# A graph and expert kernel: weights loaded during the projection, gathers of 128 rows, edge rows stored in two parts, six x buffers, the last group in halves

## What is computed

```python
h = rmsnorm(layernorm(x)) * rms_w @ W_down          # 10000 x 256
src, dst = edges + one loop per node
xl, xr = h @ Wl, h @ Wr                             # 4 heads of 64
e = sum(leaky(xl[src] + xr[dst]) * att)             # per edge and head
alpha = softmax of e over the edges with the same dst
x = x + segment_sum(alpha * xl[src], dst) @ W_up
z = layernorm(x)
w[i] = mean(top2(z @ expert_tokens.T) == i)         # 0 or 1/2 for each of 8 experts
x = x + sum_i w[i] * (gelu(gelu(z @ W1[i] + b1[i]) @ W2[i] + b2[i]) @ W3[i] + b3[i])
```

## Time and profile before

| what | us |
|---|---|
| runs shown | 1731.69, 1720.94, 1732.09 (median 1731.69) |
| profiled execution, its own time | 1720.88 |
| its span, first to last instruction | 1719.2 |
| PE busy | 1541.9 (90%) |
| DVE busy | 1201.9 (70%) |
| ACT busy | 687.1 (40%) |
| POOL busy | 692.5 (40%) |

### The profile page before, as it was taken

How to read it: one execution, slowest core, us unless ns; L and a number is a source line. 1 busy time by engine, 2 the same in 40 slices (tenths; PEclk the granted TensorE clock), 3 DMA queues, 4 the chain that set the end, 5 groups by cost and what they waited for, 6 DMA issues and landing times.

```text
span 1719.2 us, 29202 instructions
## 1 busy us (share of the span) xinstructions
PE 1541.9 (90%) x9481; PEld 1280.2 (74%) x9481; DVE 1201.9 (70%) x2392; ACT 687.1 (40%) x1365; POOL 692.5 (40%) x720
## 2 busy tenths in 40 slices
PE   6999999995697645999999992999999999999997
PEld 5999999994486334888787781777777777777775
DVE  5666666663487664887788785677777777777775
ACT  2444444442243630000000000666666666666663
POOL 1121112114677003565555536344444444444432
PEclk9999999997799886898889886999999999999999
DMA  9766566633934146799988985677666676765420
GB/s 217 214 160 166 162 174 162 152 97 90 177 104 113 60 142 154 182 238 252 251 240 243 242 254 174 206 224 219 214 210 215 208 214 205 223 198 175 128 56 15
DMA packets 136589, 306.37 MB, mean 178 GB/s; under 512 B 78543, under 2 KB 80845, under 8 KB 129067
## 3 DMA queue, kind: packets, MB, share of 16 engines
q1 hardware_dynamic: 70235, 196.21, 43.3%
q0 software_dynamic: 66208, 108.34, 21.0%
HBM read 219.78 MB, written 138.85 MB: 209 GB/s over the span
## 4 chain that ended last, share of the span: by engine, by line
PE 42%; issue 19%; DMA 19%; POOL 7%; DVE 3%; SPq 3%; ACT 2%; ACTq 0%; POOLq 0%; DVEq 0%
DMA rows_x<-cx 13%; PE psum L1845 13%; PE psum L1813 7%; PE psum L1519 7%; PE psum L1520 5%; PE psum L1521 5%; PE psum L1843 4%; POOL xls L624 2%; POOL where_from L592 2%; POOL td L628 2%; ACT xld L845 2%; DMA w_raw<-in_L_ffn_W 1%; SPq L421 1%; SPq L431 1%; POOL rstd L581 1%
## 5 line engine op out<-in xcount | busy, mean ns | idle before, releaser
L1845 PE MATMUL psum<-w_raw,gl 128*128 128x512 f32 x528 | 269.7, 592 | 0.0
L876 ACT ACTIVATE xt_hi<-psum 128x512 fp32r<-128x512 f32 x264 | 150.6, 596 | 238.3 <-PE psum L1813 238.2
L1446 DVE TENSOR_TENSOR xt_lo<-psum,xt_hi 128x512 fp32r<-128x512 f32 x264 | 176.5, 689 | 79.7 <-ACT xt_hi L876 79.7
L1558 PE MATMUL psum<-wdx_hi,axt_hi 128*125 128x272 f32 x640 | 191.5, 299 | 7.0 <-DVE wd_lo L994 4.0
L1813 PEld LDWEIGHTS psum<-ident,xn 128*128 128x128 f32 x1056 | 126.5, 142 | 94.2 <-issue 68.3
L1459 DVE SCALAR_TENSOR_TENSOR xb<-psum,xb 128x512 f32<-128x512 f32 x264 | 176.1, 687 | 28.5 <-PE psum L1845 28.4
L960 DVE TENSOR_TENSOR axt_lo<-psum,axt_hi 128x500 fp32r<-128x500 f32 x160 | 108.5, 678 | 122.8 <-ACT axt_hi L744 122.7
L1560 PE MATMUL psum<-wdx_hi,axt_lo 128*125 128x272 f32 x640 | 185.7, 290 | 0.0
L1559 PE MATMUL psum<-wd_lo,axt_hi 128*125 128x256 f32 x640 | 180.3, 282 | 0.0
L870 ACT ACTIVATE xn<-xb 128x1024 f32<-128x1024 f32 x132 | 156.1, 1233 | 53.5 <-DMA xb<-rows_x,idx_in 53.5
L716 POOL DMA_INDIRECT out<-xb,idx_in x132 | 133.6, 1012 | 106.2 <-issue 59.7
(11 more groups left out here) (277 smaller groups left out, 3944.5 us busy)
## 6 DMA issues: line engine op xcount, KB each, us to landing
rows_x<-cx SPq DMA_DIRECT2D x20, 1806.0 KB
w_raw<-in_L_ffn_W SPq DMA_DIRECT2D x140, 256.0 KB, 12.4
cx<-in_x SPq DMA_DIRECT2D x20, 1792.0 KB
ax<-in_x SPq DMA_DIRECT2D x19, 1792.0 KB
node_table<-trow SPq DMA_DIRECT2D x19, 896.0 KB
node_table<-xld SPq DMA_DIRECT2D x10, 500.0 KB
rows_x<-cx SPq DMA_DIRECT2D x20, 209.6 KB
cx<-in_x SPq DMA_DIRECT2D x20, 208.0 KB
```

What stands on the lines that cost most here:

```text
L1446: dve.tensor_tensor(xt_lo[:, 2 * q:2 * q + 2, :].rearrange("p k n -> p (k n)"), T_R[q % 2], xt_hi[:, 2 * q:2 * q + 2, :].rearrange("p k n ...
L1558: pe.matmul(into, high, wdx_hi[:, k, :], start=k == 0, stop=False, skip_group_check=True)
L1845: pe.matmul(Y[u], gl2[:, t % 2, rows], w3_raw[:, t % N3, HALF * n:HALF * (n + 1)], start=False, stop=True, skip_group_check=True).then_inc ...
```

## The change

- w1 is loaded in eight parts in groups 1 to 8 of the projection and w_up in group 9; w1 is split on ACT and DVE in groups 11 to 18, w_up in batches 4 to 7 of the edge stage, and turned in batches 0 to 3.
- All gathers of xls, td and agg take 128 rows; the index tables have 128 partitions, the three new ones hold row 0. `pad` clears what the new partitions of the buffers may hold.
- Each pass of edge rows is stored in two parts, of 112 and of 13 partitions. dst_row is loaded after half of the batches.
- Eight masks (NSM) instead of two.
- Six cx buffers (NCX) instead of three; loads 1 to 5 are issued once the first group's agg has landed; `load_cx(g + 5)` takes the place of `load_cx(g + 2)`.
- In the group stage, `ranks_in`, `place`, `slots` and `slot_numbers` of the group before come earlier.
- The last group's moments, scale, shift and store are done in two halves.
- The memset of xb goes; two columns of all eight buffers are cleared by POOL. The memset of `tail` goes.

The diff, cut to its core:

```diff
-NOLD, NR, N3 = 4, 4, 4
+NCX, NSM = 6, 8
+NR, N3 = 4, 4
 ROW = D + 8
 SLOTS = NE - 1
 LAST_PAIR = (NE - 2) * NE + NE - 1
 SENT = 520
+PADT, PADW = 16288, 17408
...
+        cx3, cx4, agg, aggt_hi, aggt_lo, cx5, c_end = run_of(
             at3,
-            ("cx1", [P, J, ROW], F32), ("cx2", [P, J, ROW], F32), ("agg", [P, 2, J, HID], F32),
-            ("aggt_hi", [128, 2, KH, G], F32R), ("aggt_lo", [128, 2, KH, G], F32R))
+            ("cx3", [P, J, ROW], F32), ("cx4", [P, J, ROW], F32), ("agg", [128, 2, J, HID], F32),
+            ("aggt_hi", [128, 2, KH, G], F32R), ("aggt_lo", [128, 2, KH, G], F32R), ("cx5", [P, J, ROW], F32))
         at_cx0 = (nc.sbuf_usable_end - origin - J * ROW * 4) // 32 * 32
-        cx = [put("cx0", [P, J, ROW], F32, at_cx0), cx1, cx2]
+        at_cx1 = at_cx0 - J * ROW * 4
+        cx = [put("cx0", [P, J, ROW], F32, at_cx0), put("cx1", [P, J, ROW], F32, at_cx1),
+              put("cx2", [P, J, ROW], F32, at4 - J * ROW * 4), cx3, cx4, cx5]
...
+            return 32 * ((NG - b + 2) // 3 + (b == (NG - 1) % 3))
...
+            sp.dma_start(pad[P:128, 0:NAX * J * D].rearrange("p (a d) -> p a d", d=D),
+                         b3_hl[P:128, :].bitcast(F32).unsqueeze(1).broadcast_to([128 - P, NAX * J, D])
+                         ).then_inc(pad_zero, 16)
...
+                if GW1 <= g < GW1 + KD:
+                    k = g - GW1
+                    sp.dma_start(w1_raw[:, :, 1, k, :],
+                                 w1[:, 128 * k:128 * (k + 1), :].rearrange("e p h -> p e h")).then_inc(raw_w1, 16)
+                if g == GW1 + KD:
+                    sp.dma_start(wup_raw[:, :, :], w_up.rearrange("(k p) n -> p k n", p=128)).then_inc(raw_wup, 16)
...
-            sp.wait_ge(setup_v, 11)
-            sp.wait_ge(sent_put, 16 * ((PAIRS + 1) * CAP // (128 * SENT)))
-            sp.dma_start(wup_raw[:, :, :], w_up.rearrange("(k p) n -> p k n", p=128)).then_inc(raw_wc, 16)
-            for k in range(KD):
-                sp.dma_start(w1_raw[:, :, 1, k, :],
-                             w1[:, 128 * k:128 * (k + 1), :].rearrange("e p h -> p e h")).then_inc(raw_wc, 16)
             for par in range(2):
                 sp.wait_ge(t_stored[par], T_STORED[par])
-            sp.wait_ge(b_xld, NBG)
+            sp.wait_ge(b_xld, NBG // 2)
...
                 sp.wait_ge(b_out, b + 1)
-                sp.dma_start(t_edge[:, bass.ds(CB * b, CB), :], xld[:, bass.ds(CB * b, CB), :]
-                             ).then_inc(rows_stored[par], 16)
+                for rows in (slice(0, SPLIT), slice(SPLIT, P)):
+                    sp.dma_start(t_edge[rows, bass.ds(CB * b, CB), :], xld[rows, bass.ds(CB * b, CB), :]
+                                 ).then_inc(rows_stored, 16)
...
+            sp.wait_ge(rows_stored, 32 * NB)
+            sp.wait_ge(agg_loaded[0], 16 * J)
+            for g in range(1, NCX):
+                load_cx(g)
+            def store_x1(g, columns, at):
+                sp.wait_ge(c_nb, at)
+                if g < NCX:
+                    sp.wait_ge(cleared, 1)
+                b = g % NCX
                 for rows in (slice(0, SPLIT), slice(SPLIT, P)):
-                    sp.dma_start(x1_g[g, rows, :], cx[b][rows, :, :].rearrange("p j d -> p (j d)")
-                                 ).then_inc(x1_put[b], 16)
+                    sp.dma_start(x1_g[g, rows, ROW * columns.start:ROW * columns.stop],
+                                 cx[b][rows, columns, :].rearrange("p j d -> p (j d)")).then_inc(x1_put[g % 3], 16)
             for g in range(NG):
-                if 1 <= g and g + 2 < NG:
+                if 1 <= g and g + NCX - 1 < NG:
                     sp.wait_ge(x1_put[(g - 1) % 3], 32 * ((g - 1) // 3 + 1))
-                    load_cx(g + 2)
-                store_x1(g)
+                    load_cx(g + NCX - 1)
+                if g < NG - 1:
+                    store_x1(g, slice(0, J), g + 1)
+                else:
+                    store_x1(g, slice(0, J // 2), g + 1)
+                    store_x1(g, slice(J // 2, J), g + 2)
...
+            pool.memset(pad[:, PADT:PADW], 0.0)
+            pool.memset(src_idx[:, :], 0)
+            pool.memset(dst_idx[:, :], 0)
+            pool.memset(from_idx[:, :, :], 0)
+            pool.memset(b3_hl[:, :].bitcast(F32), 0.0)
...
-                        out=xls[0:P, c, 0:HID], out_offset=None, in_=t_half[0:2 * N, :],
+                        out=xls[:, c, 0:HID], out_offset=None, in_=t_half[0:2 * N, :],
...
-                if t < NOLD:
-                    pool.wait_ge(r_clear, t + 1)
-                elif t < NX:
-                    pool.wait_ge(cleared, 4)
-                else:
-                    pool.wait_ge(r_clear, NOLD + t - NX + 1)
+                pool.wait_ge(r_clear, t + 1)
...
+            def high_w1(k):
+                act.wait_ge(raw_w1, 16 * KD)
+                hi, _, raw = w1_piece(k)
+                act.activation(hi, raw, ACT.Copy).then_inc(w1_hi, 1)
...
+                if i % J == 1 and 0 <= i // J - GS1 < KD:
+                    high_w1(i // J - GS1)
...
+            def low_w1(k):
+                hi, lo, raw = w1_piece(k)
+                dve.wait_ge(w1_hi, k + 1)
+                dve.tensor_tensor(lo, raw, hi.bitcast(F32), ALU.subtract)
...
+                if j == J - 1 and 0 <= g - GS1 < KD:
+                    low_w1(g - GS1)
...
-            same_segment(0, 0)
-            same_segment(1, 1)
+            for b in range(NSM):
+                same_segment(b)
...
-                if has_batch(b, 2):
-                    same_segment(b + 2, par)
+                if isinstance(b, int) and b + NSM < NB:
+                    same_segment(b + NSM)
...
-            dve.memset(tail[96:128, :], 0.0).then_inc(cleared, 1)
-            dve.memset(cx[0][:, :, D + 2:ROW], 0.0)
-            dve.wait_ge(cleared, 1)
-            dve.memset(cx[1][:, :, D + 2:ROW], 0.0)
-            dve.memset(cx[2][:, :, D + 2:ROW], 0.0).then_inc(cleared, 1)
+            dve.wait_ge(rows_stored, 32 * NB)
+            for b in range(NCX):
+                last = dve.memset(cx[b][:, :, D + 2:ROW], 0.0)
+            last.then_inc(cleared, 1)
...
                 sum_score(g)
+                if g >= 1:
+                    place(g - 1)
                 residual(g, 0)
                 greater(g)
+                if g >= 1:
+                    slots(g - 1)
                 residual(g, 1)
                 equal(g)
                 if g >= 1:
-                    bias_c(g - 1)
+                    bias_c(g - 1, slice(0, J), g)
+                    slot_numbers(g - 1)
                 bn_c(g, 0)
                 break_ties(g)
                 bn_c(g, 1)
                 residual(g, 2)
                 all_beats(g)
                 residual(g, 3)
-                if g >= 1:
-                    place(g - 1)
                 bn_c(g, 2)
                 rank_of(g)
-                if g >= 1:
-                    slots(g - 1)
                 bn_c(g, 3)
-                if g >= 1:
-                    slot_numbers(g - 1)
+                if not more:
+                    moments(g, g % 2, c_bn, c_aggr, c_var, 1.0, LN_EPS, 0, J // 2)
...
+                if not more:
+                    bias_c(g, slice(0, J // 2), NG)
...
+            moments(NG - 1, (NG - 1) % 2, c_bn, c_aggr, c_var, 1.0, LN_EPS, J // 2, J, 1)
             place(NG - 1)
-            bias_c(NG - 1)
             slots(NG - 1)
+            bias_c(NG - 1, slice(J // 2, J), NG + 1)
             slot_numbers(NG - 1)
...
-            dve.memset(xb[:, NOLD:NX, :, :], 0.0).then_inc(cleared, 1)
...
-            segment_sums(0, 0)
-            segment_sums(1, 1)
-            with pe.Fori(1, NB // 2) as i:
-                for par in range(2):
-                    segment_sums(2 * i + par, par)
+            for b in range(NB):
+                segment_sums(b, b % 2)
...
                 scores(g)
+                if g >= 1:
+                    ranks_in(g - 1)
                 for u in range(2):
                     up(g, u)
-                if g >= 1:
-                    ranks_in(g - 1)
```

212 lines of the change are left out of this document (103 added, 109 removed).

## The result

The changed kernel takes **1651.9 us** (median of 4; 1648.8 to 1653.5) where the kernel before took 1729.2 in the same comparison (median of 4; 1720.9 to 1732.1). The ratio is 0.9581, with a 95% interval from 0.9555 to 0.9608. The profiled execution took 1652.1 us, with a span of 1649.9. Against the profiled execution of before, 1720.9, that is -68.8 us; the forecast sum was -60.5. By the two medians it is 77 us.

What follows compares the result with a forecast made beforehand. It took PE to bound the projection, POOL's issue the edge gathers, and waits for stores and loads the group stage. Terms summed to -60.5, 1720.9 to 1660.4 us; a third of the gap between executions made it 1664, range 1642 to 1690.

Steps and rivals of the forecast that it cites:

- C0: Time when PE turns the first gathered rows and the group stage starts; forecast to move from 663.7 to 630 us.
- Projection: Nine more loads and w1 splits on DVE and ACT, covered by three banks of turned x: +2 us, bounds 0 to 11.
- Gathers: Edge stage: no weights' wait and 128 rows at 1.49 us a step beside DVE: -21 us, bounds -11 to -26.
- stall behind the weights: Edge gathers: POOL's idle 11.00 us while PE waits for weights would go; alone worth -11 us.
- dst_row: Edge stage: its earlier load shares engines that carry little; no separate term in the sum.
- finish: End of edge stage: eight masks made early spare six of ten passes a step: -2.5 us, bounds 0 to -3.2.
- Edge rows: Two-part store: the last edge rows land in 5 instead of 16.11 us: -11 us, bounds -7 to -14.
- rival of serialized transfers: Edge rows: the two-part store serializes and gains nothing, kernel 1675 us; chance 0.05.
- Group stage: With six buffers the lists are ready at C0 + 368 instead of C0 + 390.3: -22 us, bounds 0 to -35.
- memset: Routed stage: without xb's memset the first gather takes 1 instead of 6.09 us: -5 us, bounds -4 to -6.
- more than forecast: Group stage: balanced gathers of sixteen engines shorten the 19.03 us cycles towards 17.09, kernel 1640 to 1650 us; chance 0.11.
- slower one: Edge gathers: POOL pays more for 128 rows; at 2.6 us per gather the kernel takes 1749 us; chance 0.03.

Runs made afterwards that it cites:

- e7: Changed kernel with w_up and the eight w1 pieces loaded, split and turned in the edge stage again, as before the change: 1656.9 us, ratio 0.9621.
- e6: Changed kernel with all its indirect gathers of xls, td and agg at 126 rows instead of 128: 1656.9 us, ratio 0.9638.
- e1: Changed kernel with all gathers of xls, td and agg back at 125 rows: 1688.3 us, ratio 0.9794.
- e9: Changed kernel with the load of dst_row waiting for the last edge batch again instead of the tenth: 1651.3 us, ratio 0.9574.
- e8: Changed kernel with DVE's memset of xb[4:8] restored and POOL clearing four buffers again: 1658.0 us, ratio 0.9638.
- e2: Changed kernel with each pass of edge rows stored in one transfer of 125 partitions again: 1668.2 us, ratio 0.9673.
- e12: Kernel before the change with only the two-part store of edge rows, 112 and 13 rows, added: 1709.8 us, ratio 0.9907.
- e3: Changed kernel with six cx buffers kept but loads only two groups ahead: 1664.0 us, ratio 0.9659.
- e4: Changed kernel with SP waiting for the store before the last, so two stores in flight, and loads four groups ahead: 1647.7 us, ratio 0.9557.
- e10: Changed kernel with the last group of the group stage stored whole, its moments, scale and shift whole too: 1656.3 us, ratio 0.9608.
- e11: Changed kernel with dst_row's load after the last edge batch, two stores in flight and loads four groups ahead: 1640.9 us, ratio 0.9521.

## Why the prediction came out as it did

The forecast of 1664 was 12 us above the result, which lies inside the range. Of the 12, 3.6 are the third of the gap between executions, which the changed kernel, with 1648.8 to 1653.5, didn't need. The rest is a balance of misses, and part of its smallness is luck: up to C0 the terms came out 15 us better than forecast (C0 at 615.0, not 630), behind it 6.5 us worse. The causes are mostly the named ones, and three terms had the wrong size or the wrong owner.

- *Projection*, +2: -1.9. The cover held; PE is at 100.00 of 100 us as before. The start of the gathers differs between executions by more than that: 417.6 in e7, without the new loads, but 417.5 in e6 with them, and 414.0 to 416.3 in the others.
- *Gathers*, -21: -29.4. This is the step that was mis-sized. I took 1.49 us a step beside DVE's work, by adding the 0.20 that 125 rows lose there to the 1.29 of the only 128-row row. Measured: 0.95 + 0.30 = 1.25 alone, and 0.99 + 0.30 in the mean of the stage. The last twenty gathers, issued while DVE is busy, take 1.42 us each before and 1.00 after. So 128 rows hardly lengthen beside DVE, and the added 0.20 was the wrong part of the term. Then POOL isn't the bound any more, PE's 4.98 us a batch is. The end of the range that I had set aside, -26, was near it. The stall behind the weights, 11 of the 21, is another matter: e7 shows that nothing of it can be read once the gathers are fast. In e1, with 125 rows, early weights and the early dst_row together bring 6.3 (153.8 to 147.5), where PE waits 12.52 us behind dst_row. So the gain is mostly that of the 128 rows, and the two terms were not a sum. No run has 128 rows as the only part of the change, so its size alone stays open.
- *dst_row*, "shares engines that carry little": wrong. It costs 4 us in the changed kernel (e9) and up to 8 in other executions (e8). The share of 0.34 from 470 to 500 us before was a mean, and said nothing of what a gather meets behind one large load.
- *finish*, -2.5: -2.4. One pass is 2.64 us.
- *Edge rows*, -11: -13.1 in the profile, +16.3 when undone (e2), -14 to -16 alone (e12). The landing took 2.58, at the near end of 2.4 to 9.4; 5 was too careful. The rival of serialized transfers fell.
- *Group stage*, -22 for six buffers: -18.9. The rebuilt queue was right in its shape: the late first store, the stores queued at the end, lists at C0 + 371.4 against 368, and the engines done at C0 + 353.3 against 357. The cycles grew from 19.03 to 19.37, which the prediction had called a sign of being wrong; it cost nothing, since no engine waits for these loads any more. The owner is shared: the deeper loads carry the body of the stage (e1, e3), and the 128 rows of agg, to which I gave -1, show in its end, where 125 rows put 9.7 us back between C0 and R. What I took as given there hid the next gain: with two stores in flight the end is 7.6 to 10 us shorter still, at the same pace of the engines (e4).
- *Last group in halves*, 0: unclear, 0 to 4 (e10).
- *memset*, -5: -2.4 in the ledger, 7.2 in the trace when restored (e8). The step itself was right: the first gather takes 1.05 us. What it freed was partly taken by the stores that drain later: DVE waits 14.18 us for them.
- The rival "more than forecast" named balanced gathers, but put their gain into shorter cycles of the group stage, and these didn't shorten; the surplus lies in the edge gathers. The slower one, POOL paying more for 128 rows, fell with e1 and e6.

## What to carry to other kernels

Count the rows of every transfer, the indirect ones too: 125 rows cost more than 126 or 128, on the issuing engine as well as in landing time, and padding with a few rows that nobody reads, or a split in 112 and 13, is a cheap fix (undone in the changed kernel, they cost 36 and 16 us, by e1 and e2; the 36 include a wait behind the moved dst_row load). When two edits lift the same limit, their gains don't add: sum the stage with the next bound (here PE's 4.98 us a batch and 17.1 us a group) and not the stalls. A load that is moved earlier must be laid against the latency of what then flies beside it, even where the mean share of the DMA engines is low. And where the engines' pace is the floor of a stage, look at what still has to land behind its last group.

## What the runs showed of the hardware

- POOL's time to issue one indirect gather depends on the row count: in the mean of the 40 gathers of td, 1.31 us for 125 rows, 1.08 for 126, 0.99 for 128. It goes with the packets of POOL's queue: 66208, 53408 and 50848. The landing took 5.3, 3.7 and 3.4 us in the median.
- A store of 125 partitions (0.5 MB) landed in 16.11 us at a DMA share of 0.28, and in 2.58 when issued as 112 and 13 (e12).
- An indirect gather issued by POOL beside a DVE memset of 128x8256 fp32 took 8.77 us (e8), and 1.00 after it.
- A single load of 2.5 MB, issued in front of gathers, held their landing back until PE had waited 2.45 to 5.95 us, with 128 or 126 rows, and 12.52 us with 125.
- PE's first matmuls still took 0.65 us behind waits of 2.45 to 3.03 us, and 1.09 or 1.10 behind waits of 3.47 to 12.52, at a granted clock of 0.50. In three of the five runs with the shorter waits the clock fell to 0.50 too, shortly after.
- The last list scatter, issued behind queued stores, landed in 9.21 to 15.01 us in eight traces, and in 2.55 or 2.56 where fewer stores were queued (e3) or two were kept in flight (e4, e11).
